# A fused four-layer kernel on one core: set-up reordered after the order of its loads, input weights scaled by ScalarE, first reset gate ahead, update factor in a tile

## The reference, cut to what matters

```python
x = x + L0(x, cond)   # shared expert (silu gate) + top-2 of 8 experts (gelu), router with a term of cond
x = x + L1(x, cond)   # comes down to a gate per channel and sequence, a function of cond
x = x + L2(x, cond)   # base_down -> gelu -> base_up, each with a rank-8 part made from cond:
    c = layernorm(cond); h = gelu(c @ W1 + bias1); w = h @ W2 + bias2      # W2: 256 x 8192
    a1, b1, a2, b2 = four [B, 256, 8] parts of w
x = x + L3(x, cond)   # a GRU over the 512 tokens, h0 = cond:
    Z = sigmoid(x Wxz + H Whz + b); R = sigmoid(x Wxr + H Whr + b)
    Ht = tanh(x Wxh + (R*H) Whh + b); H = Z*H + (1-Z)*Ht; Y = H Whq + b
```

## Time and profile before

| what | value |
|---|---|
| median of 3 runs | 1224.48 us (1224.37 to 1226.22) |
| profiled execution, its own time | 1227.36 us |
| its span in the trace | 1224.8 us |
| busy in the span | PE 99%, weight loads 95%, DVE 73%, ACT 37%, POOL 5% |
| DMA | 43.8 MB, most of the weights in the first 46 us |

### The profile page before, as it was taken

One profiled execution on the slowest core, in us unless ns is written; L12 is line 12 of the kernel. 1 busy time (PEld: TensorE's weight loads), 2 busy tenths in 40 slices (PEclk: granted clock), 3 DMA queues, 4 the chain that ended last, 5 costly groups with the idle time before them and its releaser, 6 DMA issues.

```text
span 1224.8 us, 53989 instructions
## 1 busy us (share of the span) xinstructions
PE 1210.3 (99%) x22455; PEld 1168.0 (95%) x22455; DVE 892.0 (73%) x5771; ACT 448.8 (37%) x2253; POOL 65.6 (5%) x50
## 2 busy tenths in 40 slices
PE   7999999999999999999999999999999999999998
PEld 6799999999999999999999999999999999999975
DVE  4377777777777777777777777777777777777765
ACT  1233333333333333333333333333333333333332
POOL 2300000000000000000000000000000000000000
PEclk8999999999999999999999999999999999999999
DMA  9401100111100111110011100011111011111000
GB/s 352 179 25 29 29 14 18 29 29 29 29 24 9 28 29 29 29 29 7 25 29 29 29 29 16 16 29 29 30 29 29 4 29 29 29 29 25 3 7 10
DMA packets 42884, 43.83 MB, mean 36 GB/s; under 512 B 7416, under 2 KB 39424, under 8 KB 41360
## 3 DMA queue, kind: packets, MB, share of 16 engines
q1 hardware_dynamic: 40288, 38.91, 10.6%
q10 hardware_dynamic: 2128, 0.89, 0.3%
q0 software_dynamic: 224, 0.59, 0.2%
HBM read 35.70 MB, written 4.69 MB: 33 GB/s over the span
## 4 chain that ended last, share of the span: by engine, by line
PE 97%; DVE 1%; DMA 1%; ACT 0%; issue 0%; ACTq 0%; POOL 0%; DVEq 0%; POOLq 0%
PE bank L373 53%; PE gate_rh L373 31%; PE gate_z L373 12%; DMA xt<-in_xT 1%; ACT rg L755 0%; DVE rhp L1044 0%; DVE state L1060 0%; DVE zin L1054 0%; ACT zg L755 0%; POOL expn L344 0%; DVE zsum L1049 0%; DVE hin L1056 0%; DVE rh L1045 0%; DVE ge L945 0%; ACT pe_e L755 0%
## 5 line engine op out<-in xcount | busy, mean ns | idle before, releaser
L755 ACT ACTIVATE rg<-gate_rh 128x16 f32<-128x16 f32 x512 | 94.3, 184 | 455.6 <-PE gate_rh L373 455.6
L373 PEld LDWEIGHTS gate_rh<-state,whp 128*128 128x128 f16 x6144 | 233.2, 96 | 20.6 <-DVE state L1060 10.0
L373 PE MATMUL gate_rh<-state,whp 128*128 128x8 f16 x6144 | 248.1, 167 | 1.8 <-DVE state L1060 0.9
L373 PEld LDWEIGHTS gate_rh<-rhp,whp 128*128 128x128 f16 x6144 | 227.5, 96 | 14.0 <-DVE rhp L1044 8.0
L373 PE MATMUL gate_rh<-rhp,whp 128*128 128x8 f16 x6144 | 234.5, 167 | 0.6 <-DVE rhp L1044 0.3
L1044 DVE SCALAR_TENSOR_TENSOR rhp<-rg,hist 128x16 f16<-128x16 f32 x512 | 89.9, 176 | 157.1 <-ACT rg L755 144.2
L373 PE MATMUL gate_z<-state,whp 128*128 128x16 f16 x4096 | 179.7, 176 | 0.0
L755 ACT ACTIVATE zg<-zsum 128x16 f32<-128x16 f32 x512 | 110.6, 216 | 166.5 <-DVE zsum L1049 166.5
L373 PE MATMUL bank<-xt,rw 128*128 128x128 f32 x1024 | 165.9, 292 | 0.0
L373 PE MATMUL bank<-ge,rw 128*128 128x128 f32 x1024 | 165.2, 290 | 0.0
L1054 DVE TENSOR_SCALAR zin<-zg,nsscale 128x16 f32<-128x16 f32 x512 | 120.2, 235 | 55.4 <-ACT zg L755 37.7
(11 more groups left out here) (159 smaller groups left out, 1604.2 us busy)
## 6 DMA issues: line engine op xcount, KB each, us to landing
gates<-gates_t SPq DMA_DIRECT2D x30, 512.0 KB, 5.2
aw<-in_aw SPq DMA_DIRECT2D x4, 2048.0 KB, 23.7
out<-osb SPq DMA_DIRECT2D x32, 128.0 KB, 2.9
xt<-in_xT SPq DMA_DIRECT2D x30, 128.0 KB, 5.5
rw<-in_rw SPq DMA_DIRECT2D x2, 1024.0 KB, 11.1
sw<-in_sw SPq DMA_DIRECT2D x3, 512.0 KB, 7.8
wh<-in_wh SPq DMA_DIRECT2D x3, 256.0 KB, 13.2
wx<-in_wx SPq DMA_DIRECT2D x3, 256.0 KB, 20.2
```

The costliest lines, as they stand in the source:

```text
L373: return pe.matmul(o, w, x, start=start, stop=stop, skip_group_check=True)
L755: return act.activation(o, i, f, **kw)
```

## The change

Seven parts, all but the last in the set-up:

1. SP's queue takes `l1w1`, `l1w2` and `aw1`, which POOL's and ACT's queues had; `up` comes behind all of `aw2`; `wx` in the order R, Z, H.
2. PE starts on `m0` ahead of the scores of `m1`, with 1, 4 and 4 matmuls of zeros (`warm`) in front of the groups that wait for loads.
3. The third block's scores read a copy of their input, `xahead`, early in the set-up, and its first four routing operations follow early.
4. The adapter runs in four parts (`adapt(p, part)`), its second sum (`low[:, 1]`) in two halves of rows, with other work between them.
5. ACT scales `wx`; POOL doesn't any more.
6. PE's first step differs (`first_reset_gate`, `first_step`): the state's part of the reset gate comes before the adapter's last products are added, and only the reset gate is projected ahead of `r_done`. The gelu and gate multiplication of `m1`'s experts 0 to 3, and the zeroing of banks `gate_rh1` and `gate_z1`, go to the first steps of the loop.
7. In every step `zin` is made with `nsscale` as a tile [128, 16] by `scalar_tensor_tensor`, where a column of one scalar for each partition stood, with `tensor_scalar`.

```diff
             sp.dma_start(rw1[:], a["rw1"]).then_inc(l0r_in, 16)
+            sp.dma_start(l1w1[:], a["l1w1"]).then_inc(l1_in, 16)
             sp.dma_start(sw2[:], a["sw2"]).then_inc(l0o_in, 16)
+            sp.dma_start(l1w2[:], a["l1w2"]).then_inc(l1w2_in, 16)
             sp.dma_start(rw2[:], a["rw2"]).then_inc(l0o_in, 16)
+            sp.dma_start(aw1[:], a["aw1"]).then_inc(ad_in, 16)
...
-            sp.dma_start(up[:], a["up"]).then_inc(l2_in, 16)
             load_aw2(3)
             load_aw2(0)
-            for g in range(3):
+            sp.dma_start(up[:], a["up"]).then_inc(up_in, 16)
+            for g in (R, Z, H):
                 sp.dma_start(wx[:, g], a["wx"][g]).then_inc(wx_in, 16)
...
-            for g in (R, Z, H):
-                pool.tensor_scalar(wx[:, g], wx[:, g], xscale[:, g:g + 1], None, ALU.mult).then_inc(wx_scaled, 1)
...
+            def first_reset_gate():
...
+                pe.wait_ge(split_w, 1)
+                pe.wait_ge(seeded, 1)
+                recur(pr, R, 0, parts, 1)
+                recur(pr, R, 1, parts, 1)
+                recur(pr, R, 0, parts, 0)
+
+            def first_step():
+                pe.wait_ge(x3_done, 1)
+                pe.wait_ge(wx_scaled, 1)
+                project(0, R, 0)
+                project(0, R, 1).then_inc(r_done, 1)
+                pe.wait_ge(wx_scaled, 2)
+                pe.wait_ge(seeded, 2)
+                project(0, Z, 0)
+                project(0, Z, 1)
+                update_gate(0, slice(0, B)).then_inc(z_done, 1)
+                pe.wait_ge(wx_scaled, 3)
+                pe.wait_ge(rg_done, 1)
+                project(0, H, 0)
+                project(0, H, 1)
...
                     if s == 14:
                         l0_out(1, "r", (6, 7))
                         pe.wait_ge(ge03_done, count(m2, 1))
+                        if m[1] < 0:
+                            set_bits(gate_rh[1])
+                            set_bits(gate_z[1]).then_inc(bits_set, 1)
...
             scores(m0, 0)
-            scores(m1, 1, 1)
+            warm(WARM_CN)
...
             i.then_inc(setup_pe, 1)
+            warm(WARM_SHARED)
             pe.wait_ge(setup_dve, 4)
             shared_up(m0, 0)
+            warm(WARM_GATED)
             gated_up(m0, 0)
-            pe.wait_ge(l1_in, 32)
+            scores(m1, 1, 1)
+            pe.wait_ge(l1_in, 16)
...
             up_base(m0)
-            low_in_rank(g2, v_done)
-            pe.wait_ge(ge03_done, 2)
-            for t in (gate_rh[1], gate_z[1]):
-                i = mm(t[:, :], zeros[:, 0:P], zeros[:], True, True)
-            i.then_inc(bits_set, 1)
+            adapt(1, 1)
+            first_reset_gate()
+            pe.wait_ge(low_dve, 3)
             up_low(m0)
...
+            act.wait_ge(wx_in, 16 * 3)
+            for g in (R, Z, H):
+                func(wx[:, g], wx[:, g], ACT.Copy, scale=xscale[:, g:g + 1]).then_inc(wx_scaled, 1)
+            act.wait_ge(bits_set, 2)
             seed_z(0)
...
-                    dve.tensor_scalar(zin[:, :, :, 1], zg[:], -1.0, nsscale[:], ALU.add, ALU.mult)
+                    dve.scalar_tensor_tensor(zin[:, :, :, 1], zg[:], -1.0, nsscale[:], ALU.add, ALU.mult)
```

More of the change, by code:

```diff
@@ L120, in build @@
         xt = sb("xt", [P, 2, KC, TOK])
+        xahead = sb("xahead", [P, KC, TOK])
         holder = sb("holder", [P, 1])
@@ L463, in recur, with update_gate @@
                     i.then_inc(last, 1)
+            def update_gate(par, now):
+                for wpart in range(HPARTS):
+                    for half in range(KC):
+                        for k in range(KC):
+                            i = mm(z_ps[par][:, :, half, now].rearrange("p a c -> p c a"), whp[:, wpart, Z, k, half * P:(half + 1) * P],
+                                   state[:, k], False, wpart == HPARTS - 1)
+                return i
+            def first_reset_gate():
+                pr = rh_ps[0][:, 0, :, 0:B]
+                parts = state[:].rearrange("p k b a -> p k a b")
+                pe.wait_ge(st_hi, 1)
+                pe.wait_ge(st_low, 1)
+                pe.wait_ge(split_w, 1)
[17 more added lines that the diff above has]
+                project(0, H, 1)
             def step(m, par, s):
                 n = step_count(m, s)
+                if n == 1:
+                    first_step()
+                    return
                 now = slice(s * B, (s + 1) * B)
@@ L475, in step @@
                 recur(pr, R, 0, parts, 0, r_done)
[L476 to L482, removed]
-                            i = mm(z_ps[par][:, :, half, now].rearrange("p a c -> p c a"), whp[:, wpart, Z, k, half * P:(half + 1) * P],
-                                   state[:, k], False, wpart == HPARTS - 1)
-                i.then_inc(z_done, 1)
+                update_gate(par, now).then_inc(z_done, 1)
             def step_end(m, par, s):
@@ L701, in _ @@
             i.then_inc(setup_pe, 1)
-            out_shared(m0)
             out_47(m0)
+            pe.wait_ge(ahead_in, 16)
+            for k in range(KC):
+                i = mm(score_ps[0], xahead[:, k], rw[:, k], k == 0, k == KC - 1)
+            i.then_inc(scores_done, 1)
+            out_03(m0)
             pe.wait_ge(setup_dve, 8)
@@ L718, in _ @@
             i.then_inc(lowT_pe, 1)
-            spread(m1)
-            pe.wait_ge(l2_in, 32)
+            pe.wait_ge(l2_in, 16)
             mid_base(m0)
@@ L1012, in early @@
                         times_gate_part(m2, 1, s - 10, pe47_done, ge47_done)
-                    if s in (12, 13):
-                        times_gate_part(m2, 0, s - 12, pe03_done, ge03_done)
+                if has_l0 and s in (12, 13):
+                    part = times_gate_part if m[1] >= 0 else times_spread_part
+                    part(m2, 0, s - 12, pe03_done, ge03_done)
                 if has_router:
@@ L1129, in _ @@
             dve.tensor_scalar(peak[:, 3:4], peak[:, 3:4], 1.0, None, ALU.max).then_inc(peaks_dve, 1)
-            times_spread(m0, 0, pe03_done, ge03_done)
+            add_router_bias((0, 2))
+            finish_l0(m0, 0)
+            dve.wait_ge(setup_act, 2)
+            link(dve.tensor_scalar(gate2[:], l1sig[:], 0.5, 2.5, ALU.mult, ALU.add))
+            l1(m0)
             dve.wait_ge(peaks_pe, 1)
```

141 lines of the change are left out of this document (77 added, 64 removed).

## The result

The changed kernel takes 1224.03 us (median of 20 runs, 1220.38 to 1225.65), the kernel before 1227.02 (20 runs, 1224.1 to 1228.51). The ratio is 0.9974, 95% interval 0.9967 to 0.998: 3.0 us faster by the medians where 7.4 were forecast, and outside the range of the prediction. Of the miss of 6.9 us in the time, 2.5 are the kernel before itself, whose median of three stood lower than that of twenty; 4.4 are a smaller gain.

The account below looks back on a forecast made before the run. PE was taken to bound the kernel, holding 97% of the chain, with a 6.12 us input wait in the set-up. Terms: 7.8 - 0.4 = 7.4 us off, 1224.48 - 7.4 = 1217.1 us; range 1213.8 to 1220.9.

Parts of the forecast that it names:

- Start of `l1w` at 13.0: Set-up: `l1w1`'s matmuls start at 13.0 us, from 12.2 to 14.6, where they started at 19.61; 6.6 us earlier.
- the rival on the clock: New start of the set-up: clock low in part of it, 2.7 to 4 us lost, time 1220 to 1221; chance 0.12.
- Everything that PE does there stays, in another order: Set-up from `l1w1` to the first `rg`: PE's work is kept but for listed exceptions, 1.90 us off 40.34.
- The forecast of the first `rg`: End of the set-up: 13.0 + 38.2 = 51.2 us in place of 59.95.
- Little waits, 0.65 in all: PE's waits from `l1w1` to the first `rg`: only the adapter's last sum stays, 0.65 us where 0.87 stood.
- the stretch that the forecast took over as it was: Set-up, from the start of `bank<-vm,low` over DVE's add to the projection: 1.23 us, unchanged.
- new waits for loads: Set-up's long middle: new waits between engines or for loads take part of the gain, 1218.5 to 1221 us; chance 0.17.
- First step +0.95, fourth +0.43, `wx` on ACT at nothing: First loop steps: candidate's projection adds 0.95 us, zeros of two banks 0.43; ACT's scaling, done by 47.5, costs nothing.
- `zin` worth 0: Every loop step: `zin` near 0.17 for 0.23 us gains nothing, since ACT's half of `hin` releases the scan.
- The rival: Loop's ring: if DVE's half of `hin` ends last, shorter `zin` gives 10.8 us more, time 1206; chance 0.05.
- Sum: Whole kernel: second `rg` 7.8 us earlier, 0.4 given back in the loop, 7.4 us off.

Follow-up runs that it names:

- e2: The changed kernel with `zin` made by `tensor_scalar` and a column of scalars again; 1227.63 us, ratio 1.0011.
- e1: The changed kernel with each adapter run in one piece again, experts 0 to 3 of `m1` ahead of the second run; 1216.27 us, ratio 0.9925.
- e4: The kernel before with outputs 0 and 1 of each adapter run ahead of 2 and 3, nothing else; 1232.98 us, ratio 1.0055.
- e6: The kernel before with each adapter run ordered output after output, one group of 32 columns at a time; 1242.64 us, ratio 1.0129.
- e7: e1 with `zin`'s instruction issued a second time in every step, into a tile that nothing reads; 1229.87 us, ratio 1.0029.
- e5: e1 with each adapter run in two pieces cut along the sum, keeping four groups, and `aw2` loaded in the same cut; 1215.17 us, ratio 0.9911.
- e11: e5 with eight opening zeros, then 1, 2 and 2, four in a first-block step, and the first reset gate's matmuls ahead of `g`; 1216.08 us.
- e12: e5 with eight opening zeros, then 1, 4 and 4, three more ahead of the `l1w1` wait, four in a first-block step; 1216.76 us.

## Why the prediction was wrong, step by step

- **Start of `l1w` at 13.0**: right, 12.53. The clock stayed at 1.00 in the profiled execution; in e2's, whose set-up differs from this one's in nothing that PE does, it fell behind this point, as the rival on the clock had it.
- **"Everything that PE does there stays, in another order"**: this step failed. The adapter in four parts with two output groups in turn costs 3.58 us for 32 records, where 64 with four groups cost 3.6: +7.2 us. The forecast of the first `rg` was 51.2, measured 58.43. The diff shows it (the loop over `t` in `adapt` goes from four values to two), and so did the profile before, where 64 records, each written as 379 ns, fit into 3.66 us. The Trainium skill states it in "TensorEngine Tiling (Array Packing)": by its section Overview a dimension of at most 32 can be tiled four times, for a speedup of up to four. The runs agree: 218 ns a record with one group against 56 with four is 3.9 times. I costed a reordering by counting records, and never asked what the order itself gave.
- **Little waits, 0.65 in all**: too low even without the parts. In e1 the waits behind `l1w` are 3.26 us, 1.69 of them for `aw2` and 0.56 in the stretch that the forecast took over as it was, and the first `rg` is at 53.81, not 51.2. That is the rival "new waits for loads", 2.6 us of it; the change hid it under the slower adapter.
- **First step +0.95, fourth +0.43, `wx` on ACT at nothing**: right. The first two `rg` are 3.70 apart (forecast 3.93), the fourth step of the first block takes 2.59 for 2.16, ACT is through with `wx` at 51.33.
- **`zin` worth 0**: this step failed too, though the instruction's length was right. The order of the two ends, 0.05 apart, was read as the order of the two releases. What counts is when the follower may start: 0.27 behind the start of DVE's `hin`, its own semaphore in between, and 0.21 behind ACT's. DVE's came last by 0.03. The rival said 10.8 us at most; it is 4.8 (some 200 steps under 2.25 us, mean 2.182 before and 2.158 after), as only 0.02 to 0.03 could be had.
- **Sum.** -7.4 + 7.2 - 4.8 - 0.2 (first step) is -5.2; the start, 0.5 earlier than forecast, and as much more between `l1w` and the first `rg` cancel. The profiled spans differ by 6.2; single long steps, in the trace before eight with 2.5 us over the same step of the other kernel and in the trace after five with 1.2 (`zin`'s own part left out), make up the other 1.0, with 0.2 lost again behind the last `rg`. But the medians differ by 3.0 only: most executions after are slower than the profiled one. The slow places shown above, of 1.4 to 3.3 us each, are large enough for it and fit the spans and clocks of most, but that they are what the other nineteen had isn't shown. To the kernel before, whose start is slow anyway while it waits, only the second can be added.

## What to carry to other kernels

When matmuls like these, [128 x 32] by [128 x 256], alternate between four groups of output partitions, the alternation is the speed: any cut of such a loop must keep all four groups in every piece, and a change of its order has a price though no instruction is added. Where two engines' results meet in one instruction, measure from each one's start to the follower's start in steps where it is surely the last, a wait for the engine's own semaphore too, before calling either hidden. When PE's work ahead of a long load is shortened, look first where the load lands, because PE can't pass it. And where executions of one kernel differ by more than the gain that is sought, one profile isn't the kernel: here the profiled execution was the fastest of twenty.

## What the runs showed of the hardware that was not expected

- Records of [128 x 32] by [128 x 256] f32 in a row: a round over four groups takes some 220 ns, and so does one over two groups and a single record of one group (before, e4, e6).
- Executions of one kernel differ in when the clock first rises to 2.4 GHz, at 4.1 to 5.1 us in eleven profiles and at 12.5 to 16.9 in three. The clock's column writes 1.00 ahead of its first record, so e7 from 10 to 12 reads 1.00 with 11 matmuls in 2 us.
- Behind PE waits of 0.58 to 1.05 us the granted clock fell to 0.50 in some profiles (e2, e5, e11); in others it stayed at 1.00 behind waits of 0.58 (the changed kernel), 1.10 (e1) and 1.91 us (e12).
- `scalar_tensor_tensor` with a full tile took 0.18 us for 16 elements a partition, `tensor_scalar` with a pointer to a scalar 0.23, and the follower starts 0.09 and 0.14 behind. The Trainium skill's "VectorE: DVE Perf Modes", section on the perf-mode tier table, gives `tensor_scalar` twice the rate of `tensor_tensor` in fp32, at 2048 elements; at 16 the form with two tensors was the shorter, and the measurement decides here.
- With the 8 MB of `aw2` in transfers of 0.5 MB the loads ran at 384 GB/s from 20 to 43, with transfers of 2 MB at 413.
